# A decoder layer on one core: the modulation waves reach all partitions by a transfer instead of by TensorE products

## What is computed

```
t = jnp.einsum('bsd,pdf->pbsf', h, path_w[l]) + path_b[l][:, None, None, :]
mod = jnp.cos(phase[l]) + jnp.sin(phase[l])
interf = jnp.sum(t * mod[:, None, None, :], axis=0)
h = _layer_norm(h + interf, ln4_g[l], ln4_b[l])
```

## Time and profile before

| | |
|---|---|
| median of 3 runs | 950.59 us (950.4 to 955.05) |
| the profiled execution: its time | 952.84 us |
| its span, first to last instruction | 950.7 us |
| mean granted clock of PE | 0.971 |
| PE busy | 894.0 us, 94% |
| DVE busy | 677.2 us, 71% |
| ACT busy | 548.8 us, 58% |
| POOL busy | 483.7 us, 51% |

### The profile page before, as it was taken

How to read it: one execution, slowest core, us unless ns; L and a number is a source line. 1 busy time by engine, 2 the same in 40 slices (tenths; PEclk the granted TensorE clock), 3 DMA queues, 4 the chain that set the end, 5 groups by cost and what they waited for, 6 DMA issues and landing times. The chain is left out here.

```text
span 950.7 us, 19690 instructions
## 1 busy us (share of the span) xinstructions
PE 894.0 (94%) x5956; PEld 747.3 (79%) x5956; DVE 677.2 (71%) x2064; ACT 548.8 (58%) x1668; POOL 483.7 (51%) x779
## 2 busy tenths in 40 slices
PE   6999999999989999999999998679999999999894
PEld 6988888888877788888888887457678778778673
DVE  3588888888886977877787776435885766666556
ACT  3565566555774766575666646345754655563463
POOL 0254546655675646444654513512861762663466
PEclk9699999999999999999999999789999999999997
DMA  3364354443584855475474437153002002001001
GB/s 127 119 216 162 112 175 145 144 154 116 190 233 147 257 169 190 142 242 169 147 237 149 139 117 238 57 215 119 0 12 78 2 1 89 1 1 45 0 1 44
DMA packets 78788, 116.43 MB, mean 122 GB/s; under 512 B 7889, under 2 KB 41713, under 8 KB 78193
## 3 DMA queue, kind: packets, MB, share of 16 engines
q1 hardware_dynamic: 75264, 111.75, 36.1%
q10 hardware_dynamic: 3440, 3.67, 1.2%
HBM read 56.67 MB, written 17.83 MB: 78 GB/s over the span
## 5 line engine op out<-in xcount | busy, mean ns | idle before, releaser
L962 ACT ACTIVATE prob<-bank,nmax 128x128 f32<-128x128 f32 (+1 forms) x512 | 209.2, 432 | 24.7 <-DVE nmax L1103 21.9
L161 PE MATMUL bank<-w_ffn,hT 128*128 128x512 f32 x768 | 193.7, 403 | 0.8 <-POOL hT L1566 0.8
L1103 DVE CUSTOM_DVE_ANT_0 bank<-bank,mask 128x128 f32<-128x128 f32 (+1 forms) x512 | 167.9, 385 | 2.0 <-PE bank L1316 1.6
L161 PEld LDWEIGHTS bank<-w_ffn,hT 128*128 128x128 f32 x768 | 141.4, 190 | 32.6 <-POOL hT L1566 1.9
L819 POOL TENSOR_TENSOR zone<-raw,zone 128x256 fp32r<-128x256 f32 x128 | 96.4, 785 | 58.8 <-ACT zone L929 58.8
L1330 PE MATMUL bank<-ident,prob 128*128 128x128 f32 x768 | 120.7, 280 | 4.3 <-ACT probT L975 2.4
L975 ACT ACTIVATE probT<-bank 128x512 f32<-128x512 f32 x97 | 58.4, 602 | 103.3 <-PE bank L1355 93.5
L161 PE MATMUL bank<-xT,w_att 128*128 128x256 f32 x864 | 117.8, 290 | 0.2 <-DVE o L1124 0.2
L161 PEld LDWEIGHTS bank<-xT,w_att 128*128 128x128 f32 x864 | 112.8, 195 | 4.0 <-issue 0.8
L962 ACT ACTIVATION_READ_ACCUMULATOR prob<-bank,nmax 128x1 f32 x512 | 111.3, 217 | 0.0
L1663 ACT ACTIVATE ht<-bank,cols 128x128 f32<-128x128 f32 x192 | 72.2, 456 | 60.9 <-PE bank L1855 60.9
(11 more groups left out here) (123 smaller groups left out, 1566.5 us busy)
## 6 DMA issues: line engine op xcount, KB each, us to landing
q<-stage SPq DMA_DIRECT2D x192, 128.0 KB, 2.2
k<-kstage SPq DMA_DIRECT2D x48, 256.0 KB, 3.8
x<-xres SPq DMA_DIRECT2D x16, 512.0 KB, 4.2
raw<-in_ent_wT SPq DMA_DIRECT2D x32, 256.0 KB, 3.8
raw<-in_ent_pw SPq DMA_DIRECT2D x32, 256.0 KB, 4.2
raw<-in_path_w SPq DMA_DIRECT2D x8, 512.0 KB, 3.6
xres<-in_x SPq DMA_DIRECT2D x8, 512.0 KB, 3.8
xres<-x SPq DMA_DIRECT2D x8, 512.0 KB, 4.1
```

The lines of the kernel that those rows point to most:

```text
L161: ins = t.matmul(out, lhs(a, k), rhs(b, k), start=first and n == 0 and m == 0, stop=last and n == len(kts) - 1 and m == 2, skip_group_chec ...
L962: ins = s.activation(prob[:, u, c * width:(c + 1) * width], banks[u][:, c * width:(c + 1) * width], ACT.Exp, scale=-1.0, bias=nmax[:, i % ...
L1103: ins = v.tensor_tensor_reduce(scored, scored, mask[:, S - width:S], scale=-1.0, scalar=3e38, op0=ALU.add, op1=ALU.min, accum_out=nmax[:, ...
```

## The change

Nothing on PE handles the waves or the bias any more. The phases and biases are laid out as 8 rows (layer, block of 128 features) with the two paths side by side, so that DVE can add the paths' products with one more instruction. The eight chained steps work on 8 x 256 numbers, in `bias_sum` as before; the bias rows lie in `x1b`. SP issues four small loads in place of two, ahead of the weights. DVE multiplies and adds the bias rows behind the piece of `w_v`, and no longer ahead of `xT`. SP stores `mod` (two transfers) and the bias (one) to memory behind step 0's loads, and behind step 1's load of `pair` it waits for the stores of `mod` and loads `mod` back, repeated for all 128 partitions, into `modb` (1 MB). `ffn_phase` loads the bias from the new tensor `path_bias` by a load that repeats one row for all partitions.

```
@@ attention_phase
-    ROWS = NL * NP * KT
-    wave16, turns16, path_b16 = (bias_sum[0:ROWS, n * P:(n + 1) * P] for n in range(3))
+    WROWS = NL * KT
+    waves, turns = (bias_sum[0:WROWS, n * NP * P:(n + 1) * NP * P] for n in range(2))
+    path_rows = x1b[0:WROWS, 0, 0:NP * P]
@@ sync
             q.dma_start(xT_raw, xT_of[0]).then_inc(s_xT, 16)
-            q.dma_start(wave16, A["phase"]).then_inc(s_phase, 16)
-            q.dma_start(path_b16, A["path_b"].rearrange("l w (k p) -> (l w k) p", p=P)).then_inc(s_pb, 16)
+            for l in range(NL):
+                rows = slice(l * KT, (l + 1) * KT)
+                q.dma_start(waves[rows, :].rearrange("k (w p) -> k w p", w=NP), A["phase"][l * NP * KT:(l + 1) * NP * KT, :].rearrange("(w k) p -> k w p", w=NP)).then_inc(s_phase, 16)
+                q.dma_start(path_rows[rows, :].rearrange("k (w p) -> k w p", w=NP), A["path_b"][l].rearrange("w (k p) -> k w p", p=P)).then_inc(s_pb, 16)
             load_weights("w_k")
@@ sync, between(i)
+                    if i == 0 and t is first:
+                        wait_alone(q, s_mod, MOD_LINKS, s_passed)
+                        for l in range(NL):
+                            q.dma_start(A["mod"][l].rearrange("w k p -> k w p"), waves[l * KT:(l + 1) * KT, :].rearrange("k (w p) -> k w p", w=NP)).then_inc(s_mst, 16)
+                        wait_alone(q, s_pbc, 1, s_passed)
+                        q.dma_start(A["path_bias"].rearrange("l (k p) -> (l k) p", p=P), path_rows[:, 0:P]).then_inc(s_pbst, 16)
                     if i == 1 and t is first:
                         q.dma_start(pair, A["path_w"][0][0]).then_inc(s_pw, 16)
+                        wait_alone(q, s_mst, 16 * NL, s_passed)
+                        q.dma_start(modb, A["mod"].rearrange("l w k p -> (l w k p)").partition_broadcast(P).rearrange("p (n d) -> p n d", d=D)).then_inc(s_modb, 16)
@@ sync, between(3) of the first turn
-                        wait_alone(q, s_pbc, NL, s_passed)
-                        for l in range(NL):
-                            q.dma_start(A["fd"][l, 1][:, KT, :], acc[:, NP * l, :]).then_inc(s_pbst, 16)
@@ gpsimd, path
-                        g.wait_ge(s_modb, NL * NP)
+                        wait_alone(g, s_modb, 16, s_passed)
@@ scalar
-            s.wait_ge(s_modp, 1)
-            for n in range(NL * NP):
-                s.activation(modb[:, n, :], banks[MOD_BANKS[n]][:, :], ACT.Copy).then_inc(s_modb, 1)
@@ vector
-            v.wait_ge(s_pb, 16)
-            v.wait_ge(s_mod, MOD_LINKS)
-            v.tensor_tensor(path_b16, path_b16, wave16, ALU.mult).then_inc(s_pbm, 1)
             v.wait_ge(s_x0, 1)
...
             weights(QUERIES, VALUES)
+            v.wait_ge(s_pb, 16 * NL)
+            v.wait_ge(s_mod, MOD_LINKS)
+            v.tensor_tensor(path_rows, path_rows, waves, ALU.mult).then_inc(s_pbm, 1)
+            v.wait_ge(s_pbm, 1)
+            v.tensor_tensor(path_rows[:, 0:P], path_rows[:, 0:P], path_rows[:, P:2 * P], ALU.add).then_inc(s_pbc, 1)
@@ vector, step 0 of the first turn
-                    if t is first and i == 0:
-                        v.wait_ge(s_pbp, 1)
-                        for l in range(NL):
-                            v.tensor_copy(acc[:, NP * l, :], banks[BIAS_BANKS[l]][:, :]).then_inc(s_pbc, 1)
@@ tensor
-            t_.wait_ge(s_mod, MOD_LINKS)
-            for n in range(NL * NP):
-                for k in range(KT):
-                    ins = t_.matmul(banks[MOD_BANKS[n]][:, k * P:(k + 1) * P], row_of(n * KT + k), wave16,
-                                    start=k == 0, stop=k == KT - 1, skip_group_check=True)
-            ins.then_inc(s_modp, 1)
@@ tensor, the first turn
-                        if t is first and i == 0 and u == 2:
-                            t_.wait_ge(s_modb, 1)
-                        if t is first and i == 1 and u == 0:
-                            t_.wait_ge(s_pbc, NL)
-                    if t is first and i == 0:
-                        path_bias()
@@ ffn_phase, sync
-                q.dma_start(bias[:, 2 * l + 1, :], A["fd"][l, 1][:, KT, :]).then_inc(s_pbias, 16)
+                q.dma_start(bias[:, 2 * l + 1, :], A["path_bias"][l].partition_broadcast(P)).then_inc(s_pbias, 16)
```

More of the change, by code:

```diff
@@ L400, in attention_phase @@
     bias_sum = sb(ctx, "bias_sum", [P, D])
+    x1b = sb(ctx, "x1b", [P, TT, D])
     pair = raw[:, RR - 1, :, :]
-    ROWS = NL * NP * KT
-    wave16, turns16, path_b16 = (bias_sum[0:ROWS, n * P:(n + 1) * P] for n in range(3))
+    WROWS = NL * KT
+    waves, turns = (bias_sum[0:WROWS, n * NP * P:(n + 1) * NP * P] for n in range(2))
+    path_rows = x1b[0:WROWS, 0, 0:NP * P]
     eb = sb(ctx, "eb", [P, NL * ET])
@@ L427, in attention_phase @@
     xres = sb(ctx, "xres", [P, TT, D])
-    x1b = sb(ctx, "x1b", [P, TT, D])
     stats = sb(ctx, "stats", [P, TT, 6])
@@ L439, in attention_phase @@
     s_ghi, s_glo = sem("s_ghi"), sem("s_glo")
-    s_phase, s_mod, s_sin, s_modp, s_modb = sem("s_phase"), sem("s_mod"), sem("s_sin"), sem("s_modp"), sem("s_modb")
+    s_phase, s_mod, s_sin, s_mst, s_modb = sem("s_phase"), sem("s_mod"), sem("s_sin"), sem("s_mst"), sem("s_modb")
     s_pw, s_pm, s_pc, s_pst = sem("s_pw"), sem("s_pm"), sem("s_pc"), sem("s_pst")
-    s_pb, s_pbm, s_pbp, s_pbc, s_pbst = sem("s_pb"), sem("s_pbm"), sem("s_pbp"), sem("s_pbc"), sem("s_pbst")
-    MOD_BANKS = (2, 5, 6, O_BANK)
-    BIAS_BANKS = (O_BANK, 5)
+    s_pb, s_pbm, s_pbc, s_pbst = sem("s_pb"), sem("s_pbm"), sem("s_pbc"), sem("s_pbst")
     s_xb0 = sem("s_xb0")
@@ L931, in _ @@
             s.wait_ge(s_mod, MOD_LINKS - 1)
-            s.activation(wave16, wave16, ACT.Sin).then_inc(s_sin, 1)
+            s.activation(waves, waves, ACT.Sin).then_inc(s_sin, 1)
             s.wait_ge(s_xT, 16)
@@ L950, in body @@
                 if t is last_self:
+                    wait_alone(s, s_pbst, 16, s_passed)
                     wait_alone(s, s_xo, 16, s_passed)
@@ L1042, in row_bias @@
                     v.wait_ge(s_eb, 16)
-                    v.wait_ge(s_modb, NL * NP)
+                    v.wait_ge(s_mst, 16 * NL)
                 v.wait_ge(s_fraw[row % RR], 32 * (row // RR + 1))
@@ L1077, in _ @@
             M = 1.5 * 2 ** 23
-            v.wait_ge(s_phase, 16)
-            link(v.tensor_scalar(turns16, wave16, 0.5 / PI, 0.125, ALU.mult, ALU.add))
-            link(v.tensor_scalar(turns16, turns16, M, M, ALU.add, ALU.subtract))
+            v.wait_ge(s_phase, 16 * NL)
+            link(v.tensor_scalar(turns, waves, 0.5 / PI, 0.125, ALU.mult, ALU.add))
+            link(v.tensor_scalar(turns, turns, M, M, ALU.add, ALU.subtract))
             for c in (6.28125, 0.0019350051879882812, 3.0199159819385986e-07):
-                link(v.scalar_tensor_tensor(wave16, turns16, -c, wave16, ALU.mult, ALU.add))
-            link(v.tensor_scalar(wave16, wave16, PI / 4, 3.1415925, ALU.add, ALU.min))
-            link(v.tensor_scalar(wave16, wave16, -3.1415925, None, ALU.max))
+                link(v.scalar_tensor_tensor(waves, turns, -c, waves, ALU.mult, ALU.add))
+            link(v.tensor_scalar(waves, waves, PI / 4, 3.1415925, ALU.add, ALU.min))
+            link(v.tensor_scalar(waves, waves, -3.1415925, None, ALU.max))
             v.wait_ge(s_sin, 1)
-            link(v.tensor_scalar(wave16, wave16, 2 ** 0.5, None, ALU.mult))
-            v.wait_ge(s_pb, 16)
-            v.wait_ge(s_mod, MOD_LINKS)
-            v.tensor_tensor(path_b16, path_b16, wave16, ALU.mult).then_inc(s_pbm, 1)
+            link(v.tensor_scalar(waves, waves, 2 ** 0.5, None, ALU.mult))
             v.wait_ge(s_x0, 1)
@@ L1283, in _ @@
             t_.wait_ge(s_wlo, VALUES)
-            def path_bias():
-                t_.wait_ge(s_modb, NL * NP)
-                t_.wait_ge(s_pbm, 1)
-                for l in range(NL):
-                    for k in range(KT):
-                        for w in range(NP):
-                            ins = t_.matmul(banks[BIAS_BANKS[l]][:, k * P:(k + 1) * P], row_of((l * NP + w) * KT + k), path_b16,
-                                            start=k == 0 and w == 0, stop=k == KT - 1 and w == NP - 1, skip_group_check=True)
-                ins.then_inc(s_pbp, 1)
             def body(t):
@@ L1932 @@
     A["out"] = nc.dram_tensor("out", (B, S, D), F32, kind="ExternalOutput").ap()
-    for n, shape in (("x1", (B, S, D)), ("x2", (B, S, D)), ("fd", (NL, 2, P, KT + 1, D))):
+    for n, shape in (("x1", (B, S, D)), ("x2", (B, S, D)), ("fd", (NL, 2, P, KT + 1, D)), ("mod", (NL, NP, KT, P)), ("path_bias", (NL, D))):
         A[n] = nc.dram_tensor(n, shape, F32, kind="Internal").ap()
```

4 lines of the change are left out of this document (removed).

## The result

The changed kernel takes 939.19 us (median of 5 runs, 938.45 to 945.02), the kernel before 951.59 beside it (5 runs, 950.4 to 955.05): the ratio is 0.9874, with a 95% interval of 0.9842 to 0.9906. That is 12.4 us, where 9.6 were forecast.

A forecast was written before the change was run, and what follows sets the result against it. PE, busy 94% of the span, was taken as the bound. Start -2.8, step 0's bias products -7.0, clock 0 and transfers +0.2 gave -9.6 us off the median 950.59: 941.0 us, whole range 938.0 to 945.5.

The forecast's parts named there:

- Term 1: Program start: without the wave products PE's prologue starts at 11.4 in place of 14.27 us; -2.8 us, bounds -3.9 and -1.4.
- Bias instructions at nothing: DVE's two new bias-row instructions behind `w_v`, 0.7 us, are hidden by PE's first scores.
- Term 2: Step 0: path-bias products between scores and values go, and no wait for exponentials or a stack replaces them; -7.0 us.
- Term 3: PE's clock in step 0 falls at the same distance, so the values keep 5.2 us; 0, bound -2.1 us.
- Warm-up lost: Rival, chance 0.11: the removed products warmed PE's clock, so the prologue stays slow until 22.2; term 1 becomes +0.9, 944.7 us.
- Term 4: Transfers ahead of turn 1: the 1 MB `modb` load barely delays the query stacks and `path()`; +0.2 us, bounds 0 and +3.

The follow-up runs named there:

- experiment 10: Changed kernel with `modb` loaded a step earlier, plus small loads behind the weights and the chained steps off the start's path; 940.1 us, ratio 0.9866 to before.
- experiment 1: Changed kernel with the 16 wave products put back on PE ahead of the prologue, results unused; 944.8 us, ratio 0.9913 to before.
- experiment 2: Changed kernel with 16 products like the path bias's put back behind the scores of step 0, results unused; 948.58 us, ratio 0.9946 to before.
- experiment 9: Changed kernel with two 256 KB stores (from `modb`) put back on SP behind turn 0's step 3; 942.38 us, ratio 0.9894 to before.
- repeats of before: The kernel before, unchanged, run for a second and a third profile; 953.04 and 952.29 us, one execution each.
- the like profile without them: Changed kernel with the `modb` load a step earlier, ahead of `pair` and the stacks; 938.97 us, ratio 0.9836 to before.
- experiment 4: Kernel before with 1 MB of unused row-repeating loads added behind `pair` in turn 0's step 1; 952.42 us, ratio 1.0 to before.

## Why the prediction was right, and where it was off

The forecast was 941.0 in a range of 938.0 to 945.5; the time is 939.19. The median of before moved from 950.59 to 951.59 with more runs, so measured side by side the gain, 12.4 us, is 2.8 us larger than forecast. By its steps:

- **Term 1 (-2.8; bounds -3.9 and -1.4): right mechanism, -3.6.** Two sizes were off. I let every small load cost SP 0.49 us and the chain start 1.0 us later; the loads of 4 KB took 0.26 to 0.44, the two added ones put the weights back by 0.47, and the chain started 0.15 later (4.60). From the chain's first step to ACT's sine it is 2.60 us (4.60 to 7.20) against 1.94 before (4.45 to 6.39), so the wider steps cost 0.66, not 0.8 (my own addends, three times 0.155 and four times 0.1, give 0.87). And `w_q` landed at 9.0, earlier than before, so no weight was late.
- **Bias instructions at nothing: right.** The scores hide them, with 0.27 us to spare.
- **Term 2 (-7.0): right, -7.2 in the profile.** The products put back cost 6.8 us of PE and 6.6 at the turns' ends. No wait for exponentials or a stack took their place: step 1 starts 5.66 us behind the scores.
- **Term 3 (0; bound -2.1): right.** The clock fell again in step 0; the values gained 0.5, and step 1 gave 0.4 back. That it can stay up there is shown once, in experiment 10.
- **Warm-up lost: refuted for these products.** The keys take 2.9 us without the wave products and 3.0 with them. The rule that sustained matmul activity releases the clock (the Trainium skill, "TensorE: Matmul & The Clock Gate", Part 1) does not describe these products, which use 8 or 16 rows: 7.16 us of them without a gap released nothing, and the keys behind them, on 128 rows, still ran at the slow rate at first. The prologue itself agrees with the rule: its later products run fast.
- **Term 4 (+0.2; bounds 0 and +3): the step that was mis-sized, +1.2.** I had the stacks "catch up before the last". They did not. I let the data of `modb` be through by 52.6 in the times of before; it landed at 44.0, which is 54.9 there (turn 0's step 3 starts 10.9 us earlier), so it was under way beside the stacks. The wait was 2.62, 2.75 and 2.71 us in three profiles of the changed kernel against 1.38 and 1.39 in three of before, and the key stacks landed in about 3 us in place of 2.2. Moving the load a step ahead restores their 2.2. How much of the query stack's wait is the load's is less certain: with the load in place it was also 2.17, 1.85 and 1.67 (experiments 1, 2 and 9), and without it 2.19 once.
- **The missing term: -1.5 on average.** The sum has no entry for the two stores of 256 KB that the change takes from SP behind step 3. I read the diff there and costed only the loads and stores that were added. SP's timeline before, the stores and then the stack:

```profile
64.09 0.83 SPq L694 DMA_DIRECT2D fd<-xb  x2
...
67.44 1.85 SPq L628 DMA_DIRECT2D q<-stage  x3
```

With the stores, PE waits 1.6 to 1.7 us for the stack of turn 1's step 2 in both repeats of before and in experiment 9. From turn 1's first scores to its store, before takes 36.1 us on average (35.93, 36.24, 36.19) and after 34.6 (33.99, 34.90, 34.88); with stores back it is 36.11, against 34.52 in the like profile without them. Where the clock falls in turn 1, PE is late by itself and the stores cost less or nothing: experiment 4 has them and takes 34.94. So the -1.9 of the first pair is not their price as such. Between the first scores of steps 0 and 1 its before takes 10.06 us, with the clock's fall and a wait of 0.76 us for DVE, and its after 7.60; behind that the after is 0.5 us slower, 0.37 of it a wait for the same stack.

Together: -3.6 - 7.2 - 0.1 + 1.2 - 1.9 = -11.6 in this pair of profiles, and -11.5 as the mean of three on each side. Against the forecast of -9.6, term 1 makes -0.8 of the difference, term 4 +1.0, turn 1 -1.9 in this pair (-1.5 on average), and terms 2 and 3 the remaining -0.3. So part of the forecast's closeness is luck: what term 4 lacks and what the missing term would have given have opposite signs. The remaining 0.9 us between 11.5 and the medians' 12.4 was not traced to a place; spans of one kernel differ by more.

## What to carry to other kernels

Where a diff removes transfers, each of them is a term like those that it adds: look at who stands behind it on the queue. One profile shows one pattern of clock falls, and a fall can hide a wait that other executions have (two of three profiles of before had it), so a second profile of before is worth more than a third reading of the first. Before you keep products because they might warm TensorE up, look at the rate of those behind them: here products on 8 or 16 rows had done nothing for it. And a start can depend on one large load: issued in the four pieces in which it is consumed, it let PE start without a gap here.

## What the runs showed of the hardware

- `w_q` (1 MB) landed earlier when it was issued later: at 1.79, 2.70 and 3.17 us its landing took 8.2, 6.9 to 7.8 and 5.8 to 6.4 us, so it was there at 10.0, 9.6 to 10.5 and 9.0 to 9.6. Why is not settled; other loads stood ahead of it in each case. As four loads of 256 KB from 1.78 its pieces were taken up from 6.21 on.
- The 1 MB load of `modb`, which reads the same 8 KB for each of 128 partitions, landed in 4.4 to 7.9 us, no slower than `w_q`, which reads 1 MB once (5.8 to 8.2).
- Two stores of 256 KB on SP's queue 1.9, 2.0 and 2.6 us ahead of a stack of three transfers of 128 KB: the stack landed 6.6 to 6.8 us after its first issue, and PE waited for it (the repeats of before, experiment 9). With 3.4 and 5.0 us between them (the first profile of before, experiment 4) PE did not wait.
- The granted clock is printed as 1.00 while the prologue's first products run at about half rate: 14 records in 3 us, then 21 in 2.7 (experiment 1); 0.24 us each for the keys, against 0.13 for such products at full clock (1.59 us for 12, in turn 1). The rates show that level, the clock's column doesn't.
